# Moving the first pair's slots, three scatters and the third pair's scaling in the hand-written engine orders of a transformer and mixture-of-experts kernel

## The reference

```python
h = jax.nn.silu(jnp.einsum('btd,edf->betf', xn, W1))
y = jnp.einsum('betf,efd->betd', h, W2)
out = jnp.einsum('bte,betd->btd', wdense, y)
```

## Time and profile before

| | |
|---|---|
| median of three runs | 1065.08 us (1064.76 to 1065.31) |
| the profiled execution | 1067.03 us |
| its span, first to last instruction | 1065.3 us |
| mean granted clock of TensorE in it | 0.976 of full speed |
| busy TensorE, VectorE, ScalarE, GpSimd | 94%, 78%, 78%, 72% |
| end of the 32 slots, first down product of an expert block, last block | about 832, 881 and 1049 us |

### The profile page before, as it was taken

One profiled execution on the slowest core, in us unless ns is written; L12 is line 12 of the kernel. 1 busy time (PEld: TensorE's weight loads), 2 busy tenths in 40 slices (PEclk: granted clock), 3 DMA queues, 4 the chain that ended last, 5 costly groups with the idle time before them and its releaser, 6 DMA issues.

```text
span 1065.3 us, 25018 instructions
## 1 busy us (share of the span) xinstructions
PE 997.0 (94%) x7558; PEld 932.4 (88%) x7558; DVE 830.9 (78%) x2733; ACT 831.4 (78%) x1621; POOL 770.0 (72%) x1157
## 2 busy tenths in 40 slices
PE   5899999999999999999999999999998859989993
PEld 4799989999999999989999999899997759889993
DVE  6777887888888878887888788787889888953545
ACT  5878887888888888888888888888887645765582
POOL 5866877787877778777777777777766677677753
PEclk9999999999999999999999999999999878999997
DMA  4101263136314432443144315501302345667363
GB/s 140 51 1 36 55 130 60 36 75 111 59 38 96 90 59 42 99 90 60 40 100 100 63 42 122 95 8 21 100 1 80 93 130 162 178 190 219 102 182 129
DMA packets 196371, 92.81 MB, mean 87 GB/s; under 512 B 119788, under 2 KB 179187, under 8 KB 196112
## 3 DMA queue, kind: packets, MB, share of 16 engines
q1 hardware_dynamic: 190352, 81.71, 32.9%
q0 software_dynamic: 4544, 8.47, 2.3%
q10 hardware_dynamic: 1344, 1.05, 0.3%
HBM read 42.98 MB, written 31.54 MB: 70 GB/s over the span
## 4 chain that ended last, share of the span: by engine, by line
PE 72%; POOL 6%; DVE 6%; issue 5%; DMA 4%; SPq 4%; ACT 2%; DVEq 0%; POOLq 0%; ACTq 0%
PE psum L1943 19%; PE psum L1820 8%; PE psum L1822 8%; PE psum L1821 8%; PE psum L1867 6%; PE psum L1901 5%; PE psum L1873 5%; PE psum L1855 4%; PE psum L2102 4%; POOL xs L929 4%; PE psum L2086 4%; SPq L508 3%; DMA this_w<-w 2%; DVE stat L1240 1%; PE psum L1964 1%
## 5 line engine op out<-in xcount | busy, mean ns | idle before, releaser
L1026 ACT ACTIVATE s<-s,shift,rstd 128x128 f32<-128x128 f32 x496 | 203.9, 485 | 40.7 <-POOL shift L761 40.3
L1943 PE MATMUL psum<-this_w,hid 128*128 128x128 f32 x1792 | 216.5, 277 | 3.0 <-DMA this_w<-w 3.0
L1943 PEld LDWEIGHTS psum<-this_w,hid 128*128 128x128 f32 x1792 | 208.5, 193 | 4.2 <-DMA this_w<-w 4.2
L1005 ACT ACTIVATE hid<-psum,col 128x512 f32<-128x512 f32 x256 | 155.2, 683 | 2.3 <-PE psum L1822 1.7
L759 POOL TENSOR_TENSOR rstd<-var,neg_half 128x4 f32<-128x4 f32 x132 | 146.3, 1108 | 11.0
L802 POOL TENSOR_TENSOR res_a<-s,row 128x512 f32<-128x512 f32 x60 | 77.4, 1290 | 73.6 <-ACT s L1026 68.4
L1240 DVE BATCH_NORM_STATS2 stat<-s 128x6 f32<-128x128 f32 x512 | 110.0, 277 | 0.0
L756 POOL TENSOR_SCALAR shift<-mv 128x4 f32<-128x4 f32 x132 | 25.8, 195 | 100.1 <-DVE mv L1244 98.8
L1820 PE MATMUL psum<-x_hi,this_w 128*128 128x512 f32 x224 | 95.5, 426 | 1.2 <-DVE x_lo L1312 1.2
L787 POOL TENSOR_TENSOR res_f<-res_f,row 128x512 f32<-128x512 f32 x64 | 92.3, 1443 | 5.0
L2102 PE MATMUL psum<-heads,hid 128*128 x624 | 86.7, 284 | 6.8 <-ACT hid L1158 5.6
(11 more groups left out here) (270 smaller groups left out, 2761.3 us busy)
## 6 DMA issues: line engine op xcount, KB each, us to landing
xs<-pad SPq DMA_DIRECT2D x18, 975.0 KB, 8.8
feature<-xrow SPq DMA_DIRECT2D x416, 32.0 KB, 2.0
res_a<-w SPq DMA_DIRECT2D x28, 256.0 KB
xblk<-xs SPq DMA_DIRECT2D x78, 65.0 KB
row<-rows SPq DMA_DIRECT2D x8, 512.0 KB, 5.4
raw_w<-w SPq DMA_DIRECT2D x15, 256.0 KB, 3.0
this_w<-next_w SPq DMA_DIRECT2D x7, 512.0 KB, 3.2
this_qkv<-next_qkv SPq DMA_DIRECT2D x6, 384.0 KB, 2.9
```

The lines of the kernel that those rows point to most:

```text
L1005: a.activation(hid[h][:, c, :], ps(3 + h + c), ACT.Gelu, bias=col[:, bass.ds(lw * FF + (C_C1 + c), 1)]).then_inc(hid_done, 1)
L1026: ins = a.activation(dst[:, t, :], src[:, t, :], ACT.Identity, bias=shift[i][:, t:t + 1], scale=rstd[i][:, t:t + 1])
L1943: ins = t_.matmul(ps(down_bank(l, s, h))[:, t * P:(t + 1) * P], hid[h][:, c, t * P:(t + 1) * P], down[:, c, :], start=c == 0, stop=c == FF ...
```

## The change

Four places in the lists change. DVE, in the last slot, does `slots(0)` and `weights(0)` directly behind the first pair's choices, ahead of the third pair's `add_res2` and the last pair's sums and moments. POOL does three scatters of the first pair ahead of the last pair's `inv_std1`, the fourth behind it, then `stack_inv(1)` and the other twelve. ACT loads silu's table behind `token_rows(3)` and does `last_norm2(2, 0)` and `(2, 1)` behind the silus of blocks 0 and 1. DVE does `last_residual` and `add_res2(LAST, 3, h)` behind the results of blocks 0 and 1, the third pair's `stack_moments` and `stack_inv` together behind block 2 and both its `outer_residual` behind block 3. PE's and SP's lists are the same.

```diff
--- before.py
+++ after.py
@@ -942,12 +942,13 @@
                 for s in range(SLOTS):
                     slot(l, l % 2, s, l == 0, l == LAST)
 
+            for i in range(3):
+                scatter(0, i)
             inv_std1(LAST, 3, 0)
             inv_std1(LAST, 3, 1)
-            scatter(0, 0)
-            scatter(0, 1)
+            scatter(0, 3)
             stack_inv(1)
-            for i in range(2, 4 * T):
+            for i in range(4, 4 * T):
                 scatter(0, i)
             resid_f(LAST, 3, 0)
             resid_f(LAST, 3, 1)
@@ -1183,15 +1184,16 @@
             token_rows(2)
             exponentials(1)
             token_rows(3)
+            load_table(ACT.Silu, 0, gelu_table, LAYERS * SLOTS - 1)
             block_features(0)
             block_features(1)
-            last_norm2(2, 0)
-            last_norm2(2, 1)
             for b in range(N_BLOCKS):
                 silu(b)
                 if b + 2 < N_BLOCKS:
                     block_features(b + 2)
-                if b in (5, 6):
+                if b < 2:
+                    last_norm2(2, b)
+                elif b in (5, 6):
                     feature_rows(b - 1)
                 elif b in (7, 8):
                     token_tiles(4, range(2 * (b - 7), 2 * (b - 6)))
@@ -1513,13 +1515,13 @@
                     logits(0)
                     first_choice(0)
                     second_choice(0)
+                    slots(0)
+                    weights(0)
                     add_res2(l, s - 1, 0)
                     add_res1(l, s, 0)
                     add_res1(l, s, 1)
                     moments1(l, s, 0)
                     moments1(l, s, 1)
-                    slots(0)
-                    weights(0)
                     stack_moments(2)
                     stack_moments(3)
                     return
@@ -1743,20 +1745,20 @@
             moments2(LAST, 2, 1)
             last_inv(2)
             table(1)
-            for h in two:
-                last_residual(4 + h)
-                add_res2(LAST, 3, h)
             for b in range(N_BLOCKS):
                 block_result(b)
                 if COPIED <= b + COPY_LEAD < N_BLOCKS:
                     copy_weights(b + COPY_LEAD)
-                if b == 0:
+                if b < 2:
+                    last_residual(4 + b)
+                    add_res2(LAST, 3, b)
+                elif b == 2:
                     stack_moments(4)
                     stack_moments(5)
-                elif b == 1:
                     stack_inv(2)
-                elif b in (2, 3):
-                    outer_residual(2 + b)
+                elif b == 3:
+                    outer_residual(4)
+                    outer_residual(5)
                 elif b == 4:
                     sum_moments(4)
                     sum_moments(5)
```

## The result

The changed kernel takes 1071.3 us in the median of 15 runs, the kernel before 1065.31 us beside it: a ratio of 1.005, with a 95% interval of 1.0034 to 1.0066, so 3.6 to 7.0 us slower. The forecast was 1068.8 us, 3.7 us slower, range 1064.3 to 1072.2. The sign and the mechanism hold; the size is some 1.6 us short.

What follows compares the result with a forecast made beforehand. DVE, in its code order, was taken to set the pace from 844 to 900 us. Terms: 2.7 + 0.2 - 0.4 + 1.5 - 0.3 = 3.7 us, giving a median of 1068.8 us, range 1064.3 to 1072.2.

Steps and rivals of the forecast that it cites:

- late deviations: POOL's last-pair deviations come later, so DVE reaches the second pair's outer residual at 849.5 instead of 846.77: +2.7 us.
- low clock: TensorE, after some 6 us idle before the third pair's residual transposes, runs 3 us at half speed: 1.5 us lost.
- routing under POOL's residual: DVE's second-pair routing, slowed by POOL's four residual instructions, loses 3.6 us instead of 3.4: +0.2 us.
- DVE's wait for the second block gone: DVE no longer waits 0.38 us for TensorE's second block before the third pair's outer residuals: -0.4 us.
- Part A: slots(0) and weights(0) moved up on DVE: slots written 3.4 us earlier, the sums and moments queued behind +2.95 us.
- Part B: Three scatters ahead of POOL's deviations: first starts 0.30 us after the slots, deviations +3.8 us, second pair's outer residual +2.7.
- Part C: Third pair's rows scaled behind two blocks: first down product 3.0 us earlier, but TensorE then idles some 6 us for DVE.
- Early blocks count: Rival: DVE does not bind the third pair, 3.0 us gained at the first down product reach block 25; 1062.1, chance 0.12.
- From there to block 25 the chain is as before: From the third pair's router product on, router, ranks, slots, 16 scatters and load keep their lengths; shift there +3.7 us.
- Port to DVE: Rival: DVE's short instructions win the port and POOL's residual waits during second-pair routing; +0.1 us, 1065.2, chance 0.15.
- Absorbed: Rival: delays on DVE and POOL end in existing waits, and the earlier first down product gains nothing; 1065.1, chance 0.08.
- Worse: Rival: second-pair routing loses the whole 5.2 us and TensorE's clock stays low for over 6 us; 1072.2, chance 0.15.

Runs made afterwards that it cites:

- the products: Changed kernel plus 54 useless TensorE transposes where it waits 6.14 us for the third pair's outer residual; ratio 1.0039 to the kernel before.
- the early residual: Kernel before with POOL's last-pair residual moved: first half ahead of the first pair's scatters, second half behind four of them; ratio 0.9984, -1.7 us.
- C alone: Kernel before with only silu's table loaded early, third pair's rows scaled behind two blocks and DVE's third-pair work reordered; ratio 1.001, 1.1 us.
- the cut residual: Changed kernel with the last pair's four POOL residual instructions cut from 128x512 to 128x4 elements; ratio 1.0015 to the kernel before.
- A alone: Kernel before with only slots(0) and weights(0) moved up on DVE, POOL's order as before; ratio 1.0014, 1.5 us.
- the three with the early residual: Kernel before with POOL's last-pair residual moved earlier: alone 0.9984; with early table and scaling 0.9987; with 44 useless products and earlier stack moments too 0.9978.
- A and B: Kernel before with slots(0) and weights(0) moved up on DVE and three scatters ahead of POOL's deviations; ratio 1.0023, 2.4 us.

## Why the prediction was right, and where its sizes were off

The forecast's chain held link by link: late deviations, a longer wait of DVE for the split, late routing, the third pair's residual late, TensorE idle for 6 us and slow behind it. By the shifts of the first profiles of both kernels, in which the lines from the low clock on are the less certain ones, its sum of 3.7 us compares so:

| term | predicted | measured | from |
|---|---|---|---|
| late deviations, to the 2nd pair's outer residual | +2.7 | +3.27 | shift |
| routing under POOL's residual | +0.2 | +0.66 | 3.93 - 3.27 |
| DVE's wait for the second block gone | -0.4 | -0.35 | outer residual ends at +3.58 |
| transposes behind that residual | | +0.09 | TensorE's transposes at +3.67 |
| low clock | +1.5 | +1.45 | 8.05 - 6.60; 1.44 given back by the products |
| TensorE's wait for rows gone | -0.3 | -0.60 | last scatter +4.52 against +5.12 |
| behind the last scatter | 0 | +0.73 | end +5.25 against +4.52 |

- **Part A** was right: the next sums +2.97 for a predicted 2.95.
- **Part B was mis-sized in one step**: "A scatter starts 0.30 us after what it follows, as at 863.63, or 0.71 us ...; I take the smaller, because POOL is already waiting". It started 837.65 - 836.70 = 0.95 us after the weights' end. These 0.65 us cover the 0.57 that separates 3.27 from 2.7. Being already waiting does not decide the value: the scatter at 874.99, for which POOL had also waited (5.94 us), came 874.99 - 874.71 = 0.28 us after its release. The 0.95 us were seen only at the first scatter of the kernel; but being the first is not enough either, since with the early residual the first scatter (844.16) starts 0.19 us behind the instruction ahead of it. The cause stays open.
- **Routing**: that the four residual instructions would lie over the routing from end to end was right. The slow rows lose (1.74 + 1.04 + 1.18 + 1.05) - 4 x 0.22 = 4.1 us, within the bounds of 2.0 and 5.2 though over the 3.6 taken, and cutting the residual gives back 4.0. By the same count the kernel before lost 3.9 (the 1.97 of the earlier trace rows and rows of 1.30, 0.84 and 0.80 us behind it, which take 0.22, 0.17 and 0.36 elsewhere) and not 3.4, so the net of 0.2 stands. What the term lacked is the wait for the ranks: DVE waited 0.28 us there before, because its instructions ahead of the slots had been slow and covered TensorE's products; now the slow rows lie earlier and it waits 0.75. With the early residual, where no row is slow, it waits 0.74 at the same place (864.25). That cover was not named in the prediction.
- **Part C** was 0.9 us too large at the first down product: 3.0 us earlier was forecast, 2.1 were measured by shift, within the bounds of 0.7 and 3.7. (The recorded 877.84 looks like the forecast 877.9, but this execution ran 0.95 us ahead of the one from which 877.9 was worked out.) It was right in its verdict: *Early blocks count* is refuted by C alone, with 4.04 us gained at the first down product and 1.04 lost at the router.
- **Clock**: "3 us at half speed, 1.5 us lost" is met by the first profile and by the products. The second profile of the changed kernel had the low clock for longer, and 904.72 - 895.47 = 9.25 us for the same stretch, 2.65 lost: within the bounds of 0 and 3.3. In the second profile of the kernel before the stretch took 6.87 us (889.33 to 896.20), with a granted clock of 1.00, so the loss lies between 1.2 and 2.65 us, by the pair that is compared.
- **"From there to block 25 the chain is as before" was wrong.** The last scatter landed after 3.96 us instead of the 2.29 of the earlier trace rows, and TensorE waited 4.05 us for block 25:

```profile
936.79 3.96 DMA xs<-xrow,slot_i
...
940.95 1.87 DMA xblk<-xs
...
942.87 0.48 PE psum L2076
```

Block 25 is at +6.34, the end at +5.25: 1.1 us come back in the blocks behind it, 0.42 of them by the fourth pair's router product (945.39 before, 950.36 after), ahead of which TensorE had waited 0.20 us for rows once more before, at 943.33. What gives the rest back was not tried. That the longer landing makes the +0.73 of the table fits the products: there it is short again, and the end is at +2.97 with the scatter at +3.36.

- **The range**: its own bounds for routing (-1.6) and clock (-1.5) would put the low end at +0.6 and not at the +1.3 that the prediction gives, some 1065.7 us; the stated range holds that too.

*Port to DVE* fell by the slow rows and by the cut residual. The Trainium skill, "SBUF — State Buffer", section "Who interferes with whom", has a DVE instruction with two SBUF inputs contend with a GpSimd instruction that reads SBUF, and the runs agree: 1.74 us beside POOL's residual, 0.23 us without it. By the same section issue order decides who blocks; the trace does not bear that out as far as its starts show it: the DVE instruction started at 863.50, 0.37 us ahead of POOL's, and was the one that waited. *Absorbed* falls with the parts' shifts. *Worse* did not happen in its form: routing lost 4.1 and not 5.2 us, and behind the wait the granted clock was 0.50 for 3.0 us in the first profile and for 5.5 us in the second (895.5 to 901.0), not for over 6.

## What to carry to other kernels

Moving work to the front of the engine that sets the pace costs its whole length on everything queued behind it, and the gain (here 3.4 us for the slots) counts only if somebody waits for that work. Before a step is taken from an idle engine's list as free, ask which engine reads its last result: three scatters and an early product were cheap on POOL and TensorE, and DVE paid or waited all the same. What two engines do at the same time can be worth more than either order: moving POOL's residual out from under DVE's routing gave 2.95 us at the second pair's weights for no work saved, and the next wait, block 0's rows, took most of it back: -1.7 us in the runs, with an interval that reaches no change.

## What the runs showed of the hardware that was not expected

The third pair's last scatter landed after 2.3 to 2.4 us in seven profiles (both of the kernel before, A alone, the changed kernel with the useless products, the three with the early residual) and after 3.7 to 4.0 us in five (both of the changed kernel, A and B, C, the cut residual). Each of the two kernels that were profiled twice repeats its own value. The order of the transfers alone does not decide it, though: the kernel with the useless products has the changed kernel's lists on POOL and SP, and differs from it on TensorE only. What decides it stays open.

The wait of 6.14 us before the third pair's residual was the same in both profiles of the changed kernel, and the low clock behind it lasted 1.2 us longer to the router in one than in the other (9.25 against 8.05 us). And two profiles of the same kernel, equal within 0.3 us for nearly 60 us (but for one row), can part by 1.6 us behind a wait for a transfer.
